# Moving the small SBUF tensors to their places between the large ones, and leaving out a 64-byte tensor ahead of all, in a fused Mamba-and-mixture layer

## The reference

```python
# x: (16, 512, 128)
z, ssm_in = x @ Wz, x @ Win                      # 256 and 64 + 64 + 8 + 512 columns
B, C, dt_raw, X = split(ssm_in)
delta = softplus(dt_raw + dt_bias)
h_t = exp(delta_t * -exp(A_log)) * h_(t-1) + X_t * (delta_t * B_t)
y_t = h_t @ C_t + D_param * X_t
x = layernorm(x + (y * (silu(z) @ Wzg)) @ Wout)
dw1, dw2, dw3 = (route_dense(x @ P_w.T @ U.T, 3, 1.0) for U in (U1, U2, U3))   # (tokens, 12)
h = gelu(sum_e dw1[:, e] * (x @ W1[e].T))        # 128 -> 512
y = sum_e dw2[:, e] * (h @ W2[e].T) + dw3 @ b2   # 512 -> 128
x = layernorm(x + y)
```

## Time and profile before

| | |
|---|---|
| median of 3 runs | 1542.64 us (1542.53 to 1543.99) |
| the profiled execution | 1543.99 us, of which its span 1542.3 us |
| PE busy | 1525.9 us (99%) |
| PEld (weight loads) busy | 1249.7 us (81%) |
| DVE, POOL, ACT busy | 1114.9, 657.1, 598.1 us |
| mean granted TensorE clock | 0.999 |

### The profile page before, as it was taken

How to read it: one execution, slowest core, us unless ns; L and a number is a source line. 1 busy time by engine, 2 the same in 40 slices (tenths; PEclk the granted TensorE clock), 3 DMA queues, 4 the chain that set the end, 5 groups by cost and what they waited for, 6 DMA issues and landing times.

```text
span 1542.3 us, 25335 instructions
## 1 busy us (share of the span) xinstructions
PE 1525.9 (99%) x8646; PEld 1249.7 (81%) x8646; DVE 1114.9 (72%) x3113; ACT 598.1 (39%) x1360; POOL 657.1 (43%) x751
## 2 busy tenths in 40 slices
PE   8999999999999999999999999999999999999998
PEld 7778888888888888888788888878888888887886
DVE  7677776877768787686776768777686776868755
ACT  6643524425244351533525244242443515335130
POOL 6671633616245270543616336162451705436040
PEclk9999999999999999999999999999999999999999
DMA  5341312304023040321403123040230403214020
GB/s 181 100 147 29 115 45 67 100 29 133 19 75 92 29 137 15 102 72 46 120 14 123 45 63 104 29 131 21 72 95 28 138 14 97 76 39 125 15 79 7
DMA packets 81456, 114.53 MB, mean 74 GB/s; under 512 B 10144, under 2 KB 37296, under 8 KB 81328
## 3 DMA queue, kind: packets, MB, share of 16 engines
q1 hardware_dynamic: 81328, 112.92, 24.4%
HBM read 107.76 MB, written 5.13 MB: 73 GB/s over the span
## 4 chain that ended last, share of the span: by engine, by line
PE 92%; POOL 3%; DVE 1%; issue 1%; DMA 1%; SPq 1%; ACT 0%; POOLq 0%; DVEq 0%; ACTq 0%
PE exp_bank L247 22%; PE exp_bank L249 22%; PE exp_bank L248 22%; PE mix_bank L896 4%; PE mix_bank L922 3%; PE mix_bank L247 3%; PE mix_bank L249 3%; PE mix_bank L248 3%; PE mix_bank L904 3%; PE mix_bank L793 1%; PE turn_bank L1249 1%; POOL w_lo L445 1%; PE mix_bank L739 1%; PE mix_bank L1013 1%; PE mix_bank L525 1%
## 5 line engine op out<-in xcount | busy, mean ns | idle before, releaser
L1190 POOL TENSOR_TENSOR sp_lo<-fbuf,sp_hi 128x512 fp32r<-128x512 f32 (+2 forms) x201 | 243.0, 1212 | 180.2 <-ACT sp_hi L1186 109.6
L247 PE MATMUL exp_bank<-w_hi,sp_hi 128*128 128x512 f32 x768 | 304.0, 396 | 0.8 <-POOL sp_lo L1242 0.8
L247 PE MATMUL exp_bank<-sp_hi,w_hi 128*128 128x512 f32 x764 | 303.3, 397 | 0.6 <-POOL sp_lo L1190 0.4
L249 PE MATMUL exp_bank<-w_hi,sp_lo 128*128 128x512 f32 x768 | 299.7, 390 | 0.0
L248 PE MATMUL exp_bank<-w_lo,sp_hi 128*128 128x512 f32 x768 | 298.9, 389 | 0.0
L249 PE MATMUL exp_bank<-sp_hi,w_lo 128*128 128x512 f32 x764 | 298.0, 390 | 0.0
L248 PE MATMUL exp_bank<-sp_lo,w_hi 128*128 128x512 f32 x764 | 297.3, 389 | 0.0
L1289 DVE SCALAR_TENSOR_TENSOR acc<-exp_bank,dw,acc 128x128 f32<-128x128 f32 x384 | 132.3, 345 | 137.3 <-PE exp_bank L249 136.7
L1186 ACT CAST sp_hi<-fbuf 128x512 fp32r<-128x512 f32 (+2 forms) x203 | 120.0, 592 | 274.8 <-DVE fbuf L1156 219.2
L856 POOL TENSOR_TENSOR Wt<-Wt,Gh 128x512 f32<-128x512 f32 x128 | 184.7, 1444 | 21.1 <-DVE Wt L848 21.1
L247 PEld LDWEIGHTS exp_bank<-sp_hi,w_hi 128*128 128x128 f32 x764 | 143.4, 188 | 39.5 <-issue 8.9
(11 more groups left out here) (267 smaller groups left out, 2285.9 us busy)
## 6 DMA issues: line engine op xcount, KB each, us to landing
row_b<-dw_rows SPq DMA_DIRECT2D x189, 256.0 KB, 3.4
seg_b<-dA_rows SPq DMA_DIRECT2D x124, 256.0 KB, 3.5
ctd<-cum_rows SPq DMA_DIRECT2D x128, 96.0 KB, 3.2
x_in<-in_x SPq DMA_DIRECT2D x16, 256.0 KB, 2.8
result<-acc SPq DMA_DIRECT2D x15, 256.0 KB, 2.3
fbuf<-in_W1T SPq DMA_DIRECT2D x12, 256.0 KB, 4.2
acc<-in_W2T SPq DMA_DIRECT2D x5, 256.0 KB, 3.4
x_in<-in_W2T SPq DMA_DIRECT2D x5, 256.0 KB, 3.3
```

Source lines behind the costliest of these rows:

```text
L247: nc.tensor.matmul(ps, s_hi, m_hi, start=start and j == 0, stop=False, skip_group_check=onto)
L249: last = nc.tensor.matmul(ps, s_lo, m_hi, start=False, stop=stop and j == n - 1, skip_group_check=onto)
L1190: sig("xw_lo", on.tensor_tensor(lo[:, cols], wide[e % 2][:, cols], hi[:, cols].bitcast(F32), ALU.subtract))
```

## The change

It changes only the order of the `sb(...)` declarations and drops the 64-byte tensor `before_lines`. No instruction, wait, queue or shape differs; only the byte addresses in SBUF do.

```diff
-        sb("before_lines", [P, 16])
         w1_hi, w1_lo = sb("w1_hi", [P, E, HID], F32R), sb("w1_lo", [P, E, HID], F32R)
...
+        wbdt = sb("wbdt", [P, NS + H])
         wout = sb("wout", [P, NQ, D])
+        router = sb("router", [P, NR * E])
         b2_sb = sb("b2_sb", [P, NC, D])
...
         strict_r = sb("strict_r", [P, P], F32R)
+        iota_i, iota_e = sb("iota_i", [P, E], I32), sb("iota_e", [P, E])
+        bias_b, neg_a, d_b = sb("bias_b", [P, H]), sb("neg_a", [P, H]), sb("d_b", [P, H])
         x_in = sb("x_in", [P, NC, D])
...
         dt_s = sb("dt_s", [P, 6, NC * H])
+        delta, a_rows = sb("delta", [P, NC, H]), sb("a_rows", [P, H, NC])
+        a = a_rows[:, :, :].rearrange("p h c -> p c h")
+        a_hi, a_lo = sb("a_hi", [P, NC, H], F32R), sb("a_lo", [P, NC, H], F32R)
+        ends = sb("ends", [P, (NC - 1) * H])
+        total = sb("total", [P, NC * NQ])
...
         st6, mv, nrm = sb("st6", [P, NC, 6]), sb("mv", [P, NC, 2]), sb("nrm", [P, 6, NC])
-        (the same lines for delta, a_rows, a_hi, a_lo, ends, total, wbdt, router, iota_i, iota_e, bias_b, neg_a, d_b)
```

More of the change, by code:

```diff
@@ L152, in layer_program @@
         st6, mv, nrm = sb("st6", [P, NC, 6]), sb("mv", [P, NC, 2]), sb("nrm", [P, 6, NC])
[L153 to L161, removed]
         xb = [ctx.enter_context(nc.psum_tensor(f"mix_bank{n}", [P, T], F32)) for n in range(NX)]
```

## The result

The changed kernel takes 1562.65 us (median of 4 runs, 1561.91 to 1562.97); beside it the kernel before took 1542.62 us (4 runs, 1542.53 to 1543.99). The ratio is 1.0127 with an interval of 1.0113 to 1.0141: 20 us slower, where no change was forecast.

The account below looks back on a forecast made before the run. TensorE, busy 1525.9 of 1542.3 us, bounds the kernel. With every address price at nothing, 1542.3 plus 1.7 gave 1544.0 us profiled, 1.35 over the runs' median, so 1542.6; range 1539 to 1560.

Parts of the forecast that it names:

- The sum over engines other than TensorE: VectorE, GpSimd, ScalarE and DMA accesses at 32-byte-off starts: each priced at nothing, partly behind about 1 us of cover.
- TensorE at nothing: Matmul operands at new starts, 32 over 64 or 0 over 128: priced at nothing, as VectorE showed no price.
- The upper bound of 23.2 us: TensorE: 16 columns more for each matmul whose moving operand is off 64 bytes, 1.0 plus 22.2 us.
- first rival: A TensorE operand starting off 64 bytes costs time, in L896, L904, L922, L739, L793, z and BC products; 1565.8 us, chance 0.21.
- stationary loads: TensorE weight loads that start off 64 bytes, 192 of the X products among them: 4.0 us more if they set the pace.
- The weights at 0 over 128: Matmuls moving `w2` or `wx` read faster and win 12 ns each: 30 us, 1512.6 us, chance 0.15.
- A late row: `seg_b` written 32 bytes off lands later, delaying scans and TensorE; at 2 us late, 14 us longer, 1557; chance 0.07.
- The order of declarations does nothing: Whole kernel: only an address's multiple of 32 matters, so the time stays the same, 1542.6 us; the forecast itself, chance 0.57.
- the full price for all matmuls: The 23.2 us charged on every TensorE matmul with an off moving operand; some 0.07 chance, left out of the range.

Follow-up runs that it names:

- sp_64: Kernel before with 64 bytes put in ahead of `sp_hi`, moving only `sp_hi`, `sp_lo` and the small tensors behind them; 1562.42 us, ratio 1.0118.
- w2_64: Kernel before with 192 bytes ahead of `w2_hi` and 64 ahead of `wbc_hi`, so only `w2` is 64 over 256 from `sp`; 1556.96 us, 1.0084.
- mid_32_far_512: Kernel before with 32 bytes ahead of `x_in` and 480 bytes of small tensors ahead of `rows`; 1545.29 us, ratio 1.0014.
- no_pad: Kernel before with only the 64-byte tensor `before_lines` taken out, so every large tensor starts 64 bytes lower; 1543.0 us, ratio 0.9996.
- rows_256: Kernel before with `delta` and `a_rows` (256 bytes) moved ahead of `rows`; 1542.89 us, ratio 0.9995.
- rows_512: Kernel before with `delta`, `a_rows`, `a_hi` and `a_lo` (512 bytes) moved ahead of `rows`; 1543.3 us, ratio 0.9997.
- fbuf_64: Kernel before with `rows` to `acc_odd` moved by 64 bytes and `sp_hi`, `sp_lo` by 256; 1543.0 us, ratio 0.9998.
- sp_lo_64: Kernel before with 64 bytes between `sp_hi` and `sp_lo`, so only `sp_lo` is off against the weights; 1562.38 us, ratio 1.0117.
- after_256: Changed kernel with 192 bytes put in ahead of `rows`, so weights to `sp` is a multiple of 256 again; 1547.08 us, ratio 1.0023.

## Why the prediction was wrong

**The sum over engines other than TensorE: right.** VectorE, GpSimd, ScalarE and the DMAs were each taken at nothing. The timeline of DVE at the start, after the change, with `wx_hi` and `wx_lo` now at 0 over 128 and `Xd` at 0 over 64 where it read at 32:

```profile
7.64 0.42 DVE L300 CAST wx_hi<-Xd 128x512 fp32r<-128x512 f32 x1
8.09 0.69 DVE L302 TENSOR_TENSOR wx_lo<-Xd,wx_hi 128x512 fp32r<-128x512 f32 x1
```

0.42 and 0.69 us as in the earlier trace rows. The product of GpSimd, by shape, against 184.7 us and 1444 ns before:

```profile
L855 POOL TENSOR_TENSOR Wt<-Wt,Gh 128x512 f32<-128x512 f32 x128 | 184.5, 1442 | 24.4 <-DVE Wt L847 24.4
```

The DMA issues, count, KB and landing:

```profile
seg_b<-dA_rows SPq DMA_DIRECT2D x124, 256.0 KB, 3.6
ctd<-cum_rows SPq DMA_DIRECT2D x128, 96.0 KB, 3.3
```

3.6 us for `seg_b` against 3.5; the cover of 1 us ahead of the matmuls that need `Wt` is enough for that, and TensorE's idle time before them is 2.6 us in the whole kernel against 2.3.

**TensorE at nothing: the step that failed.** It looked at each operand by its own start and asked whether 32 over 64, or 0 over 128, is dearer. It took the block from `rows` to `ix`, `sp` in it, to be unchanged because its remainder over 128 stayed. The runs put another variable in its place: the distance between the moving and the stationary operand, over 256. It went from 0 to 64 for the expert matmuls and cost 12.6 + 3.2 us over their 4,595 distances, with 0.9 for the 384 of `wzg`. Subtracting two rows of the table of addresses would have shown that the distance changes. The trace could not price it, as every large pair of before stands at one distance, which is what the prediction named as able to make it wrong.

One rule of the Trainium skill was weighed there: SBUF — State Buffer, Specifications, with lines of 16 bytes. The runs show costs that it does not give: a block 64 bytes on, no line crossed that was not crossed before, is 20 us slower (sp_64). The Trainium skill says on the same page, under "Who interferes with whom", that PE never waits for anyone, and its table there gives PE one read port for the moving operand and one for the weight load and calls them independent. From that no price of a distance between the two would follow. Measured is that the time of an expert product depends on where its two operands stand to each other (w2_64, 542.7 us for one and 531.5 for the other); whether one read waits for the other, no run shows.

**The upper bound of 23.2 us: near the size by another way.** It was worked out for 1776 matmuls that start off 64 bytes (first rival, 1565.8 us). Measured is 1562.65, but L922 and L896, the largest of the groups that carried 22.2 of the 23.2 us, did not move (60.0 and 60.0; 70.8 and 70.5 us), and all plain float32 matmuls together took 0.3 us more. Of its terms only those with `xT` had something in them. The 144 that move `xT`, priced at 1.0 us, and 12 more of the first batch grew by 0.4 us in all, while the medians of their groups with `wz` rose from 227 to between 233 and 235 ns. The 192 that move `wx` and load `xT`, which stood among the stationary loads, grew by 1.2 us, and of that 0.9 us appear in sp_64 too, where `xT` did not move. mid_32_far_512, which leaves the experts at a distance of 0, costs 1.75 us. Whether that is their start or their distance of 32 over 256 to the weights was not separated. That the number comes near is chance; the rival is wrong.

**The weights at 0 over 128 (third rival, 1512.6 us): wrong.** no_pad has the weights at that start, at 1543.0 us. The gap between 227 and 215 ns, from which it was made, stands unexplained: no group of expert matmuls in any run had a median below 226 ns.

**A late row (second rival, 1557): wrong.** The idle time of TensorE fell by 0.4 us.

**The order of declarations does nothing: wrong,** though most orders do nothing: no_pad, rows_256, rows_512 and fbuf_64 all change addresses at no price. The range ended at 1560 because the full price for all matmuls was left out of it; the time lies 2.65 us above.

**Open.** Why 256 bytes; why the dear product at 64 is the one that moves `w2` and at 192 the one that moves `sp`; in what order within a row of three the price falls (sp_lo_64); and the last 3.5 us between after_256 and the kernel before, of which mid_32_far_512, with `xT` at 32 over 256 from its weights where after_256 has 160, explains about half. Plain float32 products kept their time in every run (*plain* 299.4 to 302.5), but most of their large pairs (`Wt,Xd`, `ctd,S`, `Wt,B_tok`, `CT,BT`) moved together and never changed their distance. Of those in the earlier trace rows only `wout,zg` did, to 128 over 256 after and to 224 in mid_32_far_512, at 60.0 us in both as before. So it is not shown for each of them.

## What to carry to other kernels

Where TensorE has no slack and its products are of float32r halves (here 128x512 matmuls, each with a new weight; other shapes were not measured), place the moving and the stationary operand at a distance that is a multiple of 256 bytes of a partition, and put small odd tensors behind the large ones. For a change of addresses alone, tabulate the differences between operands that one instruction reads, not only each one's own remainder. When TensorE's busy time grows with the same count and clock, read the distances from start to start by operand: the mean duration of one changed by 5 ns, the distance of 30 starts from 6.80 to 7.00 us.

## What the hardware showed that was not expected

A 128x512 float32r matmul with a new 128x128 weight takes 227 ns when all such pairs of the kernel stand at 0 over 256, and 226 to 237 ns (medians of the groups of expert matmuls) where those of its product do not. 16 bytes off cost 1.0% of this kernel, 64 and 192 cost 1.2%, 224 cost 1.7%, 96 cost 1.9%. The weight loads themselves show nothing of it, since PEld's busy time is 1249.7 us before and 1251.1 after: the price shows in the distances between the starts of matmuls, and only in part in their durations. And a pair that is off lengthens the ones beside it (231 to 233 ns for `sp_hi` against `w1` in sp_lo_64, and a median of 234 ns instead of 227 for `wx_hi,xT_hi` in sp_64, both at an unchanged distance).
